# One-token shift ahead of the local layers' feed-forwards, on the matrix engine alone

## The reference, cut to what matters

```python
def shift_token(t):
    t1, t2 = jnp.split(t, 2, axis=-1)
    t2 = jnp.pad(t2, ((0, 0), (1, 0), (0, 0)))[:, :-1]
    return jnp.concatenate([t1, t2], axis=-1)

x = x + o @ wo                       # local attention's output
h = shift_token(x)                   # the shift of this case
mu = h.mean(-1, keepdims=True); var = h.var(-1, keepdims=True)
h = (h - mu) / jnp.sqrt(var + 1e-05) * lg + lb
h = h @ w1 + b1
a, g = jnp.split(h, 2, axis=-1)
x = x + (a * gelu(g)) @ w2 + b2
```

## Time and profile before

| | us |
|---|---|
| median of 3 runs | 3964.98 (3964.82 to 3969.65) |
| the profiled execution: its time | 3962.53 |
| the profiled execution: span of the core | 3960.7 |
| mean granted PE clock, of full speed | 0.978 |

### The profile page before, as it was taken

One profiled execution on the slowest core, in us unless ns is written; L12 is line 12 of the kernel. 1 busy time (PEld: TensorE's weight loads), 2 busy tenths in 40 slices (PEclk: granted clock), 3 DMA queues, 4 the chain that ended last, 5 costly groups with the idle time before them and its releaser, 6 DMA issues. The chain is left out here.

```text
span 3960.7 us, 55447 instructions
## 1 busy us (share of the span) xinstructions
PE 3417.7 (86%) x19803; PEld 1783.7 (45%) x19959; DVE 2567.4 (65%) x5513; ACT 1771.5 (45%) x3776; POOL 990.3 (25%) x855
## 2 busy tenths in 40 slices
PE   5888898888988889888988889888898889888877
PEld 2345434444344443444344443444434444444444
DVE  5666765666567665666656665666656666576675
ACT  1454444543444535544344444445354453444424
POOL 3032311332023310333113330233203331133224
PEclk8999999999999999999999999999999999999988
DMA  4100101102011021000110020110200001100130
GB/s 163 33 12 28 39 31 33 36 4 68 2 33 38 1 69 32 12 28 34 36 33 31 8 65 4 33 38 1 69 27 18 28 30 40 33 27 13 61 89 22
DMA packets 82300, 138.66 MB, mean 35 GB/s; under 512 B 10566, under 2 KB 56808, under 8 KB 79588
## 3 DMA queue, kind: packets, MB, share of 16 engines
q1 hardware_dynamic: 75972, 120.91, 9.6%
q10 hardware_dynamic: 3744, 6.61, 0.6%
q0 software_dynamic: 2304, 7.46, 0.5%
HBM read 105.06 MB, written 29.10 MB: 34 GB/s over the span
## 5 line engine op out<-in xcount | busy, mean ns | idle before, releaser
L652 DVE TENSOR_REDUCE nmax<-banks 128x1 f32<-128x512 f32 (+3 forms) x1216 | 760.1, 658 | 391.9 <-PE banks L462 205.2
L572 ACT ACTIVATE probs<-banks 128x512 f32<-128x512 f32 (+3 forms) x1024 | 475.5, 527 | 292.7 <-PE banks L481 204.6
L462 PE MATMUL banks<-ks,qs 72*128 72x512 bf16 (+3 forms) x1536 | 440.8, 332 | 86.4 <-DVE nmax L652 61.0
L481 PE MATMUL banks<-qs,ks 74*128 74x512 bf16 (+3 forms) x1536 | 446.9, 331 | 46.8 <-ACT probs L572 17.2
L113 PE MATMUL banks<-filler,identb 128*128 128x512 bf16 x1632 | 415.9, 383 | 14.8 <-PEq L445 7.6
L462 PEld LDWEIGHTS banks<-ks,qs 72*128 72x128 bf16 x1536 | 140.9, 98 | 371.5 <-DVE nmax L652 214.6
L572 ACT ACTIVATE early<-banks 128x256 f32<-128x256 f32 (+3 forms) x512 | 194.3, 442 | 168.1 <-PE banks L481 166.7
L1518 ACT ACTIVATE probs<-banks,nm 128x192 f32<-128x192 f32 x512 | 172.1, 421 | 206.7 <-DVE nm L1470 206.7
L113 PEld LDWEIGHTS banks<-filler,identb 128*128 128x128 bf16 x1776 | 170.2, 98 | 203.5 <-issue 57.2
L531 PE MATMUL banks<-probs,v 128*32 128x512 f32 (+3 forms) x2048 | 236.2, 533 | 19.1 <-DVE att L639 10.3
L1552 POOL TENSOR_TENSOR probs<-probs,inv 128x768 f32<-128x768 f32 x128 | 187.0, 1466 | 253.6 <-DVE inv L1480 253.6
(11 more groups left out here) (523 smaller groups left out, 6659.3 us busy)
## 6 DMA issues: line engine op xcount, KB each, us to landing
qs<-parts_scratch SPq DMA_DIRECT2D x300, 96.0 KB
ks<-parts_scratch SPq DMA_DIRECT2D x288, 96.0 KB
parts_scratch<-parts SPq DMA_DIRECT2D x50, 384.0 KB, 2.5
shared<-in_w_h SPq DMA_DIRECT2D x17, 1024.0 KB, 7.9
shared<-in_w SPq DMA_DIRECT2D x26, 256.0 KB, 3.9
qs<-max_parts SPq DMA_DIRECT2D x192, 4.0 KB
xn<-in_x SPq DMA_DIRECT2D x9, 256.0 KB, 2.8
factor_scratch<-g SPq DMA_DIRECT2D x8, 256.0 KB, 2.3
```

Source lines behind the costliest of these rows:

```text
L462: mm = nc.tensor.matmul(K.ps[:, b, i * keys:(i + 1) * keys], K.qs[0:72, 4 * g + j, t * P:(t + 1) * P], K.ks[0:72, 4 * g + j, 0:keys], star ...
L481: mm = nc.tensor.matmul(K.ps[:, b, q0:T], K.ks[0:KR, h, k * P:(k + 1) * P], K.qs[0:KR, h, q0:T], start=True, stop=not on_tensor)
L572: nc.scalar.activation(probs[:, 4 * (q % QUADS) + m % 4, q0:T], K.ps[:, bank("second", m), q0:T], ACT.Exp, scale=scale).then_inc(exped, 1)
L652: nc.vector.tensor_reduce(nmax[:, t, h:h + len(heads)], K.ps[:, n % 2, 0:len(heads) * keys].rearrange("p (j k) -> p j k", k=keys), AX.X, A ...
```

## The change

The diff replaces, in `Glu`, the four turns, the two copies and the four turns back by three fp32 products into the same kind of PSUM bank. With the identity stationary the first copies features 0 to 63 of all four tiles (256 columns). With the identity shifted by one column the second moves features 64 to 127 down by one partition (256 columns). The third takes partitions 96 to 127 of tiles 0 to 2 (192 columns) with a 32 x 128 matrix that has a single one, and adds partition 127's row to partition 0 of the next tile. All three are emitted before the generator's first `yield`. The identity becomes a view, one element into a tile of 129 columns; the 32 x 128 matrix is loaded into free partitions of `w2_down[0]`, as one more of the late loads. `copy_shifted` remains for the shifts ahead of the local layers' attention.

```diff
@@ Glu.__init__
-         self.gelu_done, self.hid_ready, self.down, self.yturned, self.shifted) = K.pool[24:37]
+         self.gelu_done, self.hid_ready, self.down) = K.pool[24:35]
-        self.y_bank, self.back_bank, self.turn_bank, self.down_bank = (7, 0, 1, 6) if alone else (7, 6, 7, 6)
+        self.back_bank, self.turn_bank, self.down_bank = 6, 7, 6
-        self.shift_act, self.shift_dve = copy_shifted(nc, K, self.yturned, self.shifted, self.y_bank)
@@ Glu.tensor
-        for t in range(NT):
-            mm = nc.tensor.transpose(K.ps[:, self.y_bank, t * P:(t + 1) * P], K.y[:, t, :], K.ident[:, :])
-        mm.then_inc(self.yturned, 1)
-        yield self.BACK_STEP
-        pe.wait_ge(self.shifted, 2)
-        for t in range(NT):
-            mm = nc.tensor.transpose(K.ps[:, self.back_bank, t * P:(t + 1) * P], K.shT[:, t * P:(t + 1) * P],
-                                     K.ident[:, :])
-        mm.then_inc(self.back, 1)
+        back = K.ps[:, self.back_bank, :].rearrange("p (t d) -> p t d", t=NT)
+        nc.tensor.matmul(back[:, :, 0:64], K.ident[:, :], K.y[:, :, 0:64], start=True, stop=True)
+        nc.tensor.matmul(back[:, :, 64:P], K.shifts[:, 0:P], K.y[:, :, 64:P], start=True, stop=False)
+        nc.tensor.matmul(back[:, 1:NT, 64:P], K.first_row[:, :], K.y[96:P, 0:NT - 1, 64:P], start=False,
+                         stop=True, tile_position=(96, 0)).then_inc(self.back, 1)
@@ Glu.vector
-        self.shift_dve(dve)
@@ Glu.scalar
-        self.shift_act(act)
@@ build_kernel
-        K.ident = sb("ident", [P, P])
+        K.shifts = sb("shifts", [P, P + 1])
+        K.ident = K.shifts[:, 1:P + 1]
@@ batch_loop
+    K.first_row = K.w2_down[0][96:P, 2, :]
+    last_to_first = np.zeros((32, P), np.float32)
+    last_to_first[31, 0] = 1.0
+    late.append((K.first_row[:, :], nc.inline_tensor(last_to_first, name="first_row_c").ap()))
-        projects.insert(0, (K.ident[:, :], nc.inline_tensor(np.eye(P, dtype=np.float32), name="ident_c").ap()))
+        projects.insert(0, (K.shifts[:, :], nc.inline_tensor(np.eye(P, P + 1, 1, dtype=np.float32), name="shifts_c").ap()))
```

More of the change, by code:

```diff
@@ L2024, in __init__ @@
         super().__init__(nc, K, ctx, 1, True)
-        self.back_bank, self.turn_bank, self.up_banks = 6, 7, [(6, 7), (2, 3)]
+        self.up_banks = [(6, 7), (2, 3)]
 class GatedNorm(Beside):
```

## The result

| | before | changed |
|---|---|---|
| median of 12 runs, us | 3964.64 | 3985.89 |
| lowest and highest | 3961.53 to 3969.65 | 3974.68 to 3996.79 |
| mean granted PE clock | 0.978 in the profiled execution | 0.969 to 0.977 in the 12 runs (profiled: 0.969) |
| the profiled execution, span | 3960.7 | 3994.3 |

The ratio is 1.0053, 95% interval 1.0041 to 1.0065: slower by 21 us, where 9.0 was forecast. Two things are in the table beside the median. The changed kernel's runs spread over 22 us, the old one's over 8. And the slower a run, the lower its clock: 3974.68 us goes with 0.977, 3996.79 with 0.969. The profiled execution is one of the slow ones. The spread by itself proves little: in the three sets of 27 to 29 further runs of the old kernel that stand beside the experiments it is 11, 16 and 23 us, with clocks from 0.972 to 0.980, so the old kernel loses clock in single runs too.

The account below looks back on a forecast made before the run. It took a chain through several engines, not a full engine, to bound both places; 8 passes of 0.87 us (place A) plus 0.25 us (place B) added 9.0 us to 3964.98, giving 3974.0 us, range 3966 to 3981.

Parts of the forecast that it names:

- What bounds the kernel: Both places: no engine is full; a chain through several engines decides, and a later L1638 lengthens the block one for one.
- The price of the products: On PE at each place: 1.58 us against 0.46, less 0.03, so what stands behind the products starts 1.15 us later.
- The tile: Third product's 32-row tile stops PE 0.19 us going in and 0.16 coming back, 0.35 in all; bounds 0 and 0.70.
- Place A: Scores and mask stand behind all three products, so the row maximum and statistics come later: 0.87 us a pass.
- Place B: Statistics come early, but L1638 stands behind two bias additions that wait for later projections: 0.25 us later a pass.
- The rest: Setup's late load is covered and the identity's 4-byte start is free: 0 taken, the start bounded above at 4.5 us.
- The sum: Both places' delays over 8 passes, 8 x (0.87 + 0.25) = 9.0 us, giving 3974.0 us; chance 0.50.
- No stop for the tile: Rival at both places: the 32-row tile is taken without stopping PE, +3.3 us, 3968.3 us; chance 0.22.
- Delay absorbed: Rival: a later wait absorbs place A's delay and only place B counts, +2 us, 3967.0 us; chance 0.12.
- The shorter shift wins: Rival: statistics start with the shifted bank at both places, -6.8 us, 3958.2 us; chance 0.05.
- Twice the price: Rival: the tile's stop twice as long, +14.6 us, 3979.6, or 5 ns more per turned tile, 3978.5; chance 0.11.

Follow-up runs that it names:

- e3: Changed kernel with the third product on the full array (128 x 128 matrix) and fillers reading the mask bands: 3967.07 us, ratio 1.0013 to the old kernel.
- e2: Old kernel with only the identity as a view 4 bytes into its tile and the extra late load: 3963.19 us, ratio 0.9998.
- e1: Old kernel with only filler products ahead of the feed-forward's first turn, four in place A, two in B: 3982.56 us, ratio 1.0049.
- e7: Changed kernel with the products behind the block's first work and ACT copying features 0 to 63 instead of the first product: 3978.21 us, ratio 1.0040.
- e9: e7 with three filler products more a pass, one in place A and two in B: 3962.76 us, ratio 0.9992 to the old kernel.
- e8: e7 with the third product on the full array and fillers reading the mask bands: 3973.54 us, ratio 1.0023 to the old kernel.
- e12: e8 with five filler products more a pass, two in place A and three in B: 3961.95 us, ratio 0.9992 to the old kernel.
- e10: Old kernel with eight filler products ahead of the first turn in each place, 3.40 us a pass: 4013.59 us, ratio 1.0118.
- e4: Old kernel with the three products in place A alone, identity and late load as changed, place B's shift as before: 3983.57 us, ratio 1.0053.

## Why the prediction was wrong, by its own steps

- **What bounds the kernel.** Right: in both places the chain ends in L1597, and what moves it moves the block. The line's 0.96 us for each us of delay and the passes with the same clock say that it is passed on.
- **The price of the products.** 1.15 us was forecast for what stands behind them; it is 1.10 (scores at +1.56 against +0.46). The products hold PE for 1.56 us where 1.58 was summed, and the 0.03 for the old group's start came on top; the runs don't show the terms one by one.
- **The tile.** Forecast 0.35 us, measured 0.30 to 0.34 by e3. Read in the prediction's way, the third product's first column comes 0.21 us after the second's last (338.49 to 338.70), where about 0.2 was forecast. The rule of the Trainium skill that it was weighed with (TensorEngine Tiling (Array Packing), Key Properties: changing the tiling mode drains the engine) agrees with that.
- **Place A.** Forecast +0.87, measured +0.70. Besides the 0.05 (1.10 and not 1.15), the distance from the row maximum to the statistics is 0.61 in the changed kernel (339.77 to 340.38), not the 0.71 taken from before.
- **Place B.** Forecast +0.25, measured +0.28, and for the reason given: the statistics 0.45 us sooner, spent in front of two additions.
- **The rest** (late load, the 4-byte start): forecast 0; e2 shows nothing beyond its interval, which is -4 to +3 us.
- **The sum.** 8 x 0.98 = 7.8 us against 9.0 forecast; at equal clock the line puts the changed kernel 6.9 us above the old one.
- **The step that failed** is in the first part: I read the granted clock as 1.00 in two stretches of the first pass and took durations as fixed from then on. There is no term for the clock in the sum and no rival in which a delay costs clock elsewhere. The trace of before had the sign, which I didn't read: its passes last 462.13 to 466.23 us with the same work. The missing term is (0.9770 - 0.9723) x 3.13 us per 0.001 = 14.7 us; with the delay's 7.5 that is 22.2, against 21.7 between the means.
- **The rivals.** No stop for the tile: out by e3. Delay absorbed: out by the distances in all passes and by the line. The shorter shift wins: the statistics did come sooner in place B, and that gave nothing; in place A they came later. Twice the price: no.

So of theory 1 this much is shown: the delay is passed on, and the rest of the time is granted clock, which is lost without any of the change's instructions (e1) and comes back with filler products alone (e7 against e9, e8 against e12). That the length of a gap doesn't decide is shown at one block border. That the moment does is argued from there, and which moments are bad is open; the version by which the length of a pass decides failed in e10.

## What to carry to other kernels

Read how long the passes of a loop are, and the granted clock of each, before pricing anything: if equal work takes different times, a small change can cost several times its own length through the clock (0.70 us a pass, 5.6 in all, cost 20 us in e4), and a shortening can cost too. Judge such a change by the distance between two instructions in all passes, and its runs at equal clock; compare against a pure delay of the same size before blaming an instruction. And what is put at the head of a block stands ahead of the first scores of all others: the same three products behind them (one `yield`) cost nothing that the runs can tell.

## What the runs showed of the hardware

- The granted clock is what separates runs of one kernel here: 3974.68 us at 0.977 and 3996.79 us at 0.969 for the same program, 3961.01 at 0.980 and 3996.79 at 0.968 for `e4_a_only`. The Trainium skill (TensorE: Matmul & The Clock Gate, Part 1) says that the gate's judging is free-running and not reset by the kernel's start, so that it varies from run to run. The traces fit that and don't prove it: at one and the same gap of 1.7 us the clock fell in 3 of the changed kernel's 8 passes. The page puts the penalty of the clock's ramp under 1% of a typical kernel's span. Here the clock's difference between the two kernels is 0.4% and twice the change's own cost; all that a mean clock of 0.977 costs against 1.000 is by an estimate from the line's slope 23 x 3.13 = 72 us, 1.8%, more than the page's figure.
- Three useless products of 0.21 us more in each pass made the kernel 15 us faster (e7 to e9).
- A product in a 32-row tile between products of the full array costs 0.30 us of PE here (1.56 against 1.26 us from the first product to the scores), the change in and the change back together. In the kernel with ACT's copy (e7 against e8) the same edit moved the next turn by 0.20 us only.
- An identity that starts 4 bytes into its tile turns 128 x 128 fp32 tiles in 283 ns; at the tile's start it was 284.
